# Splitting the two VectorE instructions of a gate chunk into two jobs of the written order

## The reference, cut to what matters

```python
def _L0_ffn_ref(x, w_gate, w_up, w_down):
    wg = _dequant(w_gate, x.dtype); wu = _dequant(w_up, x.dtype); wd = _dequant(w_down, x.dtype)
    gate = jnp.einsum('bsd,hd->bsh', x, wg)
    up = jnp.einsum('bsd,hd->bsh', x, wu)
    h = jax.nn.silu(gate) * up
    return jnp.einsum('bsh,dh->bsd', h, wd)
x = L0_attn_a_x                                        # 8 batches x 256 rows x 128, fp32
x = x + _L0_attn_a_ref(_layernorm(x, axis=-1), ...)    # spike-timing attention, sigmoid projections
x = x + _L0_ffn_ref(_layernorm(x, axis=-1), ...)       # "F": 128 -> 384 -> 128, int weights / 127
x = x + _L0_attn_b_ref(_layernorm(x, axis=-1), ...)    # causal softmax attention, 16 heads of 64
x = x + _L0_ffn_ref(_layernorm(x, axis=-1), ...)       # "P": the same weights again
return x
```

## Time and profile before

| what | us |
|---|---|
| median of 3 runs | 320.98 |
| lowest and highest | 320.28, 321.02 |
| span of the profiled execution | 318.3 |
| TensorE busy (matmuls, modelled ends) | 307.6 |
| TensorE weight loads | 268.4 |
| VectorE busy | 278.0 |
| ScalarE busy | 248.9 |
| GpSimd busy | 227.9 |

### The profile page before, as it was taken

The page is one execution under the profiler, slowest core; times in us unless marked ns, Lnnn a source line. Parts: engine busy times, 40 slices in busy tenths (PEclk is TensorE's granted clock), DMA queues, the critical chain, the costliest instruction groups (busy, mean ns, idle before and its releaser), DMA issues.

```text
span 318.3 us, 10097 instructions
## 1 busy us (share of the span) xinstructions
PE 307.6 (97%) x3186; PEld 268.4 (84%) x3186; DVE 278.0 (87%) x1117; ACT 248.9 (78%) x848; POOL 227.9 (72%) x305
## 2 busy tenths in 40 slices
PE   6898999999999999999999999999999999999995
PEld 5687987988888898898888897888978998888884
DVE  4698999999899989997999989989998898998564
ACT  2665599899779798869889886998779788779832
POOL 4465786949978976977995489863977497646740
PEclk9999999999999999999999999999999999999999
DMA  7900000000000000000000000000000000000001
GB/s 201 316 7 0 3 0 4 2 3 1 2 2 2 2 2 4 0 3 3 18 2 3 3 16 3 2 18 3 2 1 4 19 0 21 2 2 4 2 0 49
DMA packets 6419, 5.83 MB, mean 18 GB/s; under 512 B 864, under 2 KB 5856, under 8 KB 6368
## 3 DMA queue, kind: packets, MB, share of 16 engines
q1 hardware_dynamic: 6080, 4.99, 5.2%
q10 hardware_dynamic: 288, 0.20, 0.2%
HBM read 4.15 MB, written 1.05 MB: 16 GB/s over the span
## 4 chain that ended last, share of the span: by engine, by line
PE 72%; POOL 13%; issue 7%; DVE 5%; DMA 1%; ACT 1%; POOLq 0%; DVEq 0%; ACTq 0%
PE bank L606 10%; PE bank L399 8%; PE bank L400 7%; PE bank L583 7%; PE bank L401 7%; PE bank L571 7%; POOL prob L1019 6%; PE bank L568 4%; PE bank L469 3%; PE bank L459 3%; PE bank L460 2%; PE bank L417 2%; PE bank L448 2%; PE bank L526 2%; PE bank L527 2%
## 5 line engine op out<-in xcount | busy, mean ns | idle before, releaser
L1019 POOL TENSOR_TENSOR prob<-prob,row_inv 128x256 f32<-128x256 f32 (+1 forms) x128 | 103.5, 838 | 33.9 <-DVE row_inv L921 33.8
L719 ACT ACTIVATE prob<-neg_s,neg_max 128x256 f32<-128x256 f32 x128 | 64.1, 501 | 0.0
L717 ACT ACTIVATE prob<-neg_s,neg_max 128x128 f32<-128x128 f32 x128 | 50.8, 397 | 13.8 <-DVE neg_max L897 13.2
L897 DVE CUSTOM_DVE_ANT_0 neg_s<-bank,mask 128x256 f32<-128x256 f32 x128 | 53.7, 420 | 0.0
L606 PE MATMUL bank<-early,v 128*64 128x256 f32 (+1 forms) x512 | 46.0, 330 | 0.1
L606 PEld LDWEIGHTS bank<-early,v 128*64 128x64 f32 x512 | 32.2, 137 | 13.1 <-issue 3.4
L931 DVE TENSOR_TENSOR qk<-bank,bqk 128x512 f32<-128x512 f32 x64 | 42.0, 681 | 0.9 <-PE bank L401 0.8
L571 PE MATMUL bank<-qk 64*128 64x256 f32 x256 | 38.6, 377 | 0.0
L895 DVE CUSTOM_DVE_ANT_0 neg_s<-bank,mask 128x128 f32<-128x128 f32 x128 | 36.4, 284 | 1.8 <-PE bank L571 1.7
L399 PE MATMUL bank<-rt_hi,wqkv_hi 128*128 128x256 f32 x128 | 37.2, 290 | 0.1
L400 PE MATMUL bank<-rt_hi,wqkv_lo 128*128 128x256 f32 x128 | 36.1, 282 | 0.0
(11 more groups left out here) (178 smaller groups left out, 887.2 us busy)
## 6 DMA issues: line engine op xcount, KB each, us to landing
early<-wqkv_in SPq DMA_DIRECT2D x3, 512.0 KB, 6.9
x<-x_in SPq DMA_DIRECT2D x8, 128.0 KB, 5.7
out<-x SPq DMA_DIRECT2D x8, 128.0 KB, 1.8
wo<-wo_in SPq DMA_DIRECT2D x1, 512.0 KB, 7.0
wa<-wa_in ACTq DMA_DIRECT2D x1, 192.0 KB, 3.1
first<-wg_in SPq DMA_DIRECT2D x1, 192.0 KB, 3.1
first<-wu_in SPq DMA_DIRECT2D x1, 192.0 KB, 3.1
first<-wd_in SPq DMA_DIRECT2D x1, 192.0 KB, 4.8
```

The lines of the kernel that those rows point to most:

```text
L717: nc.scalar.activation(prob[:, r, e, 0:P], neg_s[:, m % SCORE_BUFS, e, 0:P], ACT.Exp, bias=neg_max[:, q, 2 * e:2 * e + 1], scale=-1.0, acc ...
L719: nc.scalar.activation(prob[:, r, e, P:SC], neg_s[:, m % SCORE_BUFS, e, P:SC], ACT.Exp, bias=neg_max[:, q, 2 * e + 1:2 * e + 2], scale=-1. ...
L897: nc.vector.tensor_tensor_reduce(out=neg_s[:, m % SCORE_BUFS, e, P:SC], in0=S[:, P:SC], in1=mask[:], scale=-SCORE_SCALE, scalar=3e38, op0= ...
L1019: nc.gpsimd.tensor_tensor(pr, pr, inv, ALU.mult).then_inc(p_norm, 1)
```

## The change

In VectorE's order each `g` job that held both instructions becomes a `g` job with the first and a `u` job with the second. The first increments a semaphore of its own (`silu_s`, one for each feed-forward and chunk), and the `u` job waits for that in place of `link`. For 26 chunks `u` follows its `g` directly. For 18 the first half of another gate chunk, where one followed, now stands between the two halves (`gF1.2 gF2.2 uF1.2 uF2.2`), and for 4 (`gF2.1`, `gP0.0`, `gP2.4`, `gP1.4`) a reciprocal that followed. Nothing else in this order moves, and the orders of the other engines stay as they are.

```diff
-        gF1.0 gF2.0 w0.0 sign.1 lntA.2 ...
+        gF1.0 uF0.0 gF2.0 uF1.0 uF2.0 w0.0 sign.1 lntA.2 ...
-        lntF.1 mask.2 qk.3 qk.4 qk.5 inverse.0 gF2.1 inverse.1 gF1.1 gF0.1 mask.3 ...
+        lntF.1 mask.2 qk.3 qk.4 qk.5 inverse.0 gF2.1 inverse.1 uF2.1 gF1.1 gF0.1 uF1.1 uF0.1 mask.3 ...
-        inverse.9 sum.5 lntF.2 qk.12 sum.7 qk.13 qk.14 gF1.2 gF2.2 mask.12 inverse.10 gF0.2 mask.13 ...
+        ... qk.14 gF1.2 gF2.2 uF1.2 uF2.2 mask.12 inverse.10 gF0.2 uF0.2 mask.13 ...
-        ... mask.19 pt1.16 gF1.3 gF0.3 sum.15 qk.20 qk.21 gF2.3 qk.22 ...
+        ... mask.19 pt1.16 gF1.3 gF0.3 uF1.3 uF0.3 sum.15 qk.20 qk.21 gF2.3 uF2.3 qk.22 ...
-        ... gP0.3 gF0.6 dbP.2 qk.43 pt1.38 pt1.39 inverse.41 gF2.6 gF1.6 sum.37 ...
+        ... gP0.3 gF0.6 uP0.3 uF0.6 dbP.2 qk.43 pt1.38 pt1.39 inverse.41 gF2.6 gF1.6 uF2.6 uF1.6 sum.37 ...
-        ... gP1.4 inverse.51 gF2.7 gF0.7 gF1.7 pt1.48 ...
+        ... gP1.4 inverse.51 uP1.4 gF2.7 gF0.7 uF2.7 gF1.7 uF0.7 uF1.7 pt1.48 ...
...
-        gate_s = {k: [sem(f"gate_s_{k}{c}") for c in range(FC)] for k in "FP"}
+        gate_s, silu_s = ({k: [sem(f"{n}_{k}{c}") for c in range(FC)] for k in "FP"} for n in ("gate_s", "silu_s"))
...
                     h = hid[buffers(k, b)][:, c, :]
-                    link(nc.vector.scalar_tensor_tensor(h, gate_t[buffers(k, b)][:, c, :], 1.0, src[:, 0:N], ALU.add, ALU.mult))
+                    nc.vector.scalar_tensor_tensor(h, gate_t[buffers(k, b)][:, c, :], 1.0, src[:, 0:N], ALU.add, ALU.mult).then_inc(silu_s[k][c], 1)
+                elif job[0] == "u":
+                    k, c = job[1], int(job[2])
+                    src, _, free = home(f"g{k}{c}", b)
+                    dve.wait_ge(silu_s[k][c], b + 1)
+                    h = hid[buffers(k, b)][:, c, :]
                     nc.vector.tensor_tensor(h, h, src[:, N:2 * N], ALU.mult).then_inc(free, 1)
```

More of the change, by code:

```diff
@@ L113 @@
         lnsA.0 ga.0 xnA.0 lnsA.1 lntA.0 gb.0 mean.0 sign.0 lntA.1 w4.0 wf.0 aout.0 lnsF.0 lnsA.2 xnF.0 bv.0 lntF.0 mean.1 gF0.0
-        gF1.0 gF2.0 w0.0 sign.1 lntA.2 dbF.0 lnsB.0 w2.0 xnB.0 lnsA.3 lntB.0 aout.1 lnsF.1 bo.0 qk.0 qk.1 qk.2 mask.0 mask.1
-        lntF.1 mask.2 qk.3 qk.4 qk.5 inverse.0 gF2.1 inverse.1 gF1.1 gF0.1 mask.3 inverse.2 mask.4 mask.5 inverse.3 qk.6 mean.2
-        qk.7 dbF.1 pt1.0 pt1.1 pt1.2 inverse.4 lnsB.1 pt1.3 mask.6 sign.2 mask.7 lntB.1 lntA.3 aout.2 inverse.5 sum.1 sum.3
@@ L117 @@
[L117 to L136, removed]
+        gF1.0 uF0.0 gF2.0 uF1.0 uF2.0 w0.0 sign.1 lntA.2 dbF.0 lnsB.0 w2.0 xnB.0 lnsA.3 lntB.0 aout.1 lnsF.1 bo.0 qk.0 qk.1 qk.2
@@ new lines @@
+        mask.0 mask.1 lntF.1 mask.2 qk.3 qk.4 qk.5 inverse.0 gF2.1 inverse.1 uF2.1 gF1.1 gF0.1 uF1.1 uF0.1 mask.3 inverse.2
+        mask.4 mask.5 inverse.3 qk.6 mean.2 qk.7 dbF.1 pt1.0 pt1.1 pt1.2 inverse.4 lnsB.1 pt1.3 mask.6 sign.2 mask.7 lntB.1
+        lntA.3 aout.2 inverse.5 sum.1 sum.3 inverse.6 qk.8 lnsF.2 inverse.7 qk.9 qk.10 qk.11 pt1.4 pt1.5 pt1.6 pt1.7 mask.8
+        mask.9 mask.10 mask.11 inverse.8 lnsA.4 inverse.9 sum.5 lntF.2 qk.12 sum.7 qk.13 qk.14 gF1.2 gF2.2 uF1.2 uF2.2 mask.12
@@ new lines @@
+        inverse.10 gF0.2 uF0.2 mask.13 mean.3 inverse.11 pt1.8 pt1.9 lnsA.5 sign.3 qk.15 dbF.2 inverse.12 inverse.13 lnsB.2
+        pt1.10 pt1.11 sum.9 mask.14 mask.15 pt1.12 lntB.2 otr.0 aout.3 lnsP.0 sum.11 lntA.4 qk.16 qk.17 lnsF.3 pt1.13 mask.16
+        inverse.14 mask.17 qk.18 lntP.0 inverse.15 inverse.16 lntF.3 qk.19 sum.13 gP2.0 uP2.0 pt1.14 pt1.15 mask.18 inverse.17
+        mask.19 pt1.16 gF1.3 gF0.3 uF1.3 uF0.3 sum.15 qk.20 qk.21 gF2.3 uF2.3 qk.22 inverse.18 pt1.17 lntA.5 mask.20 mask.21
@@ new lines @@
+        inverse.19 gP1.0 uP1.0 dbF.3 lnsB.3 gP0.0 inverse.20 uP0.0 mask.22 pt1.18 pt1.19 otr.1 lntB.3 mean.4 inverse.21 qk.23
+        qk.24 qk.25 lnsP.1 inverse.22 sign.4 pt1.20 mask.23 pt1.21 mask.24 lnsA.6 sum.17 mask.25 inverse.23 aout.4 lntP.1 sum.19
+        sum.21 inverse.24 lnsF.4 gP2.1 uP2.1 qk.26 qk.27 pt1.22 pt1.23 pt1.24 mask.26 mask.27 lntF.4 qk.28 inverse.25 qk.29
+        lnsA.7 gP1.1 uP1.1 qk.30 qk.31 mask.28 inverse.26 gF1.4 uF1.4 mean.5 gF0.4 uF0.4 pt1.25 gF2.4 uF2.4 sum.23 inverse.27
@@ new lines @@
+        sign.5 lntA.6 gP0.1 uP0.1 sum.25 dbP.0 dbF.4 inverse.28 lnsB.4 mask.29 mask.30 otr.2 lnsP.2 inverse.29 pt1.26 pt1.27
+        mask.31 inverse.30 lntB.4 aout.5 lnsF.5 sum.27 qk.32 qk.33 pt1.28 pt1.29 pt1.30 mask.32 mask.33 lntF.5 inverse.31 qk.34
+        qk.35 gF2.5 gF0.5 uF2.5 uF0.5 mask.34 mask.35 pt1.31 qk.36 qk.37 inverse.32 inverse.33 inverse.34 gF1.5 uF1.5 lntP.2
+        mask.36 mask.37 sum.29 sum.31 inverse.35 lntA.7 pt1.32 pt1.33 qk.38 qk.39 gP0.2 uP0.2 dbP.1 gP2.2 uP2.2 dbF.5 inverse.36
@@ new lines @@
+        lnsB.5 inverse.37 pt1.34 pt1.35 mean.6 gP1.2 uP1.2 otr.3 sign.6 lnsP.3 sum.33 pt1.36 pt1.37 lntB.5 sum.35 mask.38
+        mask.39 aout.6 lnsF.6 qk.40 qk.41 lntP.3 mask.40 inverse.38 inverse.39 mask.41 inverse.40 lntF.6 qk.42 gP0.3 gF0.6 uP0.3
+        uF0.6 dbP.2 qk.43 pt1.38 pt1.39 inverse.41 gF2.6 gF1.6 uF2.6 uF1.6 sum.37 pt1.40 pt1.41 sum.39 mask.42 mask.43 qk.44
+        qk.45 gP1.3 uP1.3 dbF.6 lnsB.6 mask.44 inverse.42 inverse.43 mask.45 gP2.3 uP2.3 mean.7 qk.46 qk.47 inverse.44
+        inverse.45 lntB.6 mask.46 otr.4 pt1.42 sign.7 pt1.43 pt1.44 lnsP.4 mask.47 sum.41 qk.48 aout.7 qk.49 lnsF.7 pt1.45
@@ L137 @@
+        mask.48 mask.49 inverse.46 inverse.47 lntP.4 qk.50 qk.51 lntF.7 gP2.4 inverse.48 uP2.4 pt1.46 pt1.47 gP0.4 uP0.4 sum.43
+        sum.45 inverse.49 mask.50 mask.51 dbP.3 sum.47 qk.52 qk.53 inverse.50 gP1.4 inverse.51 uP1.4 gF2.7 gF0.7 uF2.7 gF1.7
+        uF0.7 uF1.7 pt1.48 pt1.49 mask.52 mask.53 otr.5 pt1.50 lnsP.5 qk.54 pt1.51 qk.55 dbF.7 lnsB.7 mask.54 mask.55 inverse.52
         inverse.53 lntB.7 dbP.4 sum.49 sum.51 lntP.5 qk.56 qk.57 inverse.54 inverse.55 qk.58 pt1.52 pt1.53 mask.56 mask.57
-        pt1.54 inverse.56 pt1.55 gP0.5 qk.59 mask.58 pt1.56 sum.53 sum.55 qk.60 qk.61 inverse.57 inverse.58 qk.62 mask.59
@@ L139 @@
-        mask.60 mask.61 qk.63 inverse.59 inverse.60 gP2.5 pt1.57 pt1.58 mask.62 inverse.61 mask.63 pt1.59 otr.6 inverse.62
-        lnsP.6 inverse.63 gP1.5 pt1.60 pt1.61 pt1.62 pt1.63 lntP.6 out0.7 out1.7 lnsP.7 gP1.6 xnP.7 gP0.6 lntP.7 gP2.6 gP0.7
-        gP2.7 gP1.7 dbP.5 dbP.6 dbP.7
+        pt1.54 inverse.56 pt1.55 gP0.5 uP0.5 qk.59 mask.58 pt1.56 sum.53 sum.55 qk.60 qk.61 inverse.57 inverse.58 qk.62 mask.59
+        mask.60 mask.61 qk.63 inverse.59 inverse.60 gP2.5 uP2.5 pt1.57 pt1.58 mask.62 inverse.61 mask.63 pt1.59 otr.6 inverse.62
@@ L142 @@
+        lnsP.6 inverse.63 gP1.5 uP1.5 pt1.60 pt1.61 pt1.62 pt1.63 lntP.6 out0.7 out1.7 lnsP.7 gP1.6 uP1.6 xnP.7 gP0.6 uP0.6
+        lntP.7 gP2.6 uP2.6 gP0.7 uP0.7 gP2.7 uP2.7 gP1.7 uP1.7 dbP.5 dbP.6 dbP.7
     """,
```

## The result

The changed kernel takes 322.08 us (median of 5 runs, 321.95 to 322.13) against 321.02 (320.28 to 321.18) for the kernel before in the same comparison. The ratio is 1.0039, with a 95% interval of 1.0028 to 1.0050: slower by 1.06 us, where +1.1 was forecast (322.1). The main term came as written down. Two smaller terms did not, and the runs of before turned out to have a spread of their own, for which two traces suggest a cause.

The account below looks back on a forecast made before the run. TensorE, nearly without holes from 30 to 300 us, was taken as the bound. Start 0.21, batch 1 -0.10, batch 2 0.87 and batch 6 0.16 sum to +1.14 us, on 320.98 giving 322.1, range 320.5 to 323.0.

Parts of the forecast that it names:

- TensorE is full from 30 to 300 us, and what it loses stays lost: TensorE, 268.86 busy of 270 us: no spare time afterwards, so any delay is kept to the end.
- A covered wait saves 0.11 us: VectorE gate chunks: 0.45 us between dependent halves against 0.34 back to back; ideal saving 2.3 us in all.
- the rival that took it for the path: No saving at all: first halves start 0.45 apart, not 0.34; +0.44 over four places, 322.5 us; chance 0.05.
- Side by side chunks cost nothing: The 26 chunks whose two jobs stay adjacent on VectorE: only the semaphore's name changes, cost zero.
- Batch 2, +0.87, through hid_hi, hid_lo and wo_lo: The main term: uF1.2 behind gF2.2 runs 0.87 us later, delaying hid_hi, hid_lo, wo_lo and TensorE's otA.0 by 0.87.
- a wait of about 1.1 before L526: Expected sign in TensorE's profile: this wait grows to about 1.1 us from 0.28, the longest of the middle.
- Batch 6, +0.16 at gP1.3: uF2.6 0.34 later delays hid_hi, zt_hi, zt_lo and VectorE's mask; less 0.18 slack, TensorE's gP1.3 loses 0.16 us.
- Start, +0.21: Batch 0 F chunks: VectorE's block ends at 24.14, past w0's start at 23.93; +0.21 us on the path, bounds 0 and 0.21.
- Batch 1, -0.10: Three chunks with tanh long ready save 0.3 us on VectorE at 43 us; -0.1 taken, bounds 0 and -0.3.
- new waits elsewhere of over 0.3: Sign that the prediction is wrong: TensorE gets waits above 0.3 us in places not forecast.
- The absorbed case: Rival: after late otA.0, small holes close, batch 1 saving counts, gP1.3 term may vanish; +0.4, 321.4 us; chance 0.28.
- the case of more late banks: Rival: two more bank delays of 0.2 and the batch 3 lag of 0.23; +1.8, 322.8 us; chance 0.10.

Follow-up runs that it names:

- e5: Only the two batch 6 pairs (P0.3 with F0.6, F2.6 with F1.6) interleaved, all other chunks side by side; 321.11 us, ratio 1.0017 to the kernel before.
- e1: Changed kernel with both halves of all 48 chunks side by side again, new semaphores kept; 320.91 us, ratio 1.0005 to the kernel before.
- e2: Only the batch 2 pair F1.2, F2.2 interleaved, the other 46 chunks side by side; 321.70 us, ratio 1.0037 to the kernel before.
- e4: Changed kernel with GpSimd's job ol.0, which makes wo_lo, moved ahead of norm.8; 321.03 us, ratio 1.0016 to the kernel before.
- e11: Changed kernel, all pairs interleaved, with wo_lo made early and VectorE's sign.7 moved behind pt1.44; 320.14 us, ratio 0.9994 to the kernel before.
- e3: Changed kernel with only F1.2 and F2.2 put back side by side; 321.08 us, ratio 1.0014 to the kernel before.
- e6: Changed kernel with VectorE's job sign.7 moved behind pt1.43 and pt1.44; 321.26 us, ratio 1.0021 to the kernel before.
- e9: Only the three chunks of batch 0 interleaved, all else side by side; 320.40 us, ratio 1.0000 to the kernel before.
- e8: Side by side except three groups (F2.1 with a reciprocal, F1.1 with F0.1, F2.5 with F0.5), wo_lo early, sign.7 late; 319.31 us, ratio 0.9962 to before.
- e10: All second halves side by side, wo_lo made early, sign.7 behind pt1.44; 319.48 us, ratio 0.9974 to the kernel before.
- e7: All second halves side by side, GpSimd's wo_lo job moved ahead of norm.8; 319.97 us, ratio 0.9976 to the kernel before.

## Why the prediction was right, point by point

- *TensorE is full from 30 to 300 us, and what it loses stays lost.* Right. In the changed kernel otA.0 stands 0.85 late and dnF.6, 140 us on, 0.88 late (1.12 and 1.15 less 0.27).
- *A covered wait saves 0.11 us.* Right. Two halves in a row are shown as 0.72 to 0.75 us of VectorE for both, which is 0.33 and one whole duration (211.46 in e5). The Trainium skill's rule (VectorE: DVE Perf Modes, section "The DRAIN you can't avoid") that leaving out waits in a chain gains nothing does not hold here (0.33 to 0.34 us from start to start in place of 0.45), and the rival that took it for the path is out. That the saving reaches nobody was right too.
- *Side by side chunks cost nothing.* Right (e1).
- *Batch 2, +0.87, through hid_hi, hid_lo and wo_lo.* Right: 0.87 alone (e2), gone when wo_lo is moved (e4). The sign "a wait of about 1.1 before L526" came as 0.77, because TensorE's jobs in front of it came 0.35 late: the delay by the bank, which the prediction rightly put inside the new wait, shortens the wait that is seen. That this delay is a cost of its own once wo_lo is out of the way (e4, e11) it did not say.
- *Batch 6, +0.16 at gP1.3.* The place and the chain were right, the size was short: 0.16 to 0.18 at gP1.3's first matmul, and 0.07 to 0.08 more before its second (0.20 us after the first, where before it was 0.12), in each kernel with these pairs (dnF.6 to qk.46: 0.25 in the changed kernel, 0.25 in e3, 0.24 in e5). Another 0.1 comes at gP1.4 in e3, e4, e5 and the changed kernel, and not in e6 and e11, which have the same pairs and no meeting at sign.7; so it seems to need both, and what makes it stays open.
- *Start, +0.21.* Wrong. VectorE's block did end later, but the lower bound held. These are its lines after:

```profile
23.42 0.42 DVE L881 SCALAR_TENSOR_TENSOR hid_F<-gate_t_F,bank 128x256 f32<-128x256 f32 x1 [0.36 <-ACT gate_t_F L666]
23.75 0.75 DVE L887 TENSOR_TENSOR hid_F<-hid_F,bank 128x256 f32<-128x256 f32 x2
24.42 0.76 DVE L822 TENSOR_TENSOR wqkv_lo<-early,wqkv_hi 128x512 fp32r<-128x512 f32 x1
25.10 1.76 DVE L892 SCALAR_TENSOR_TENSOR less<-less,dist 128x512 f32<-128x512 f32 x1
```

w0 starts 0.49 later than in the earlier trace rows, 0.22 of it from the change, and takes 0.76 in place of 0.97; sign.1 starts 0.28 later, which is the shift of the first microseconds alone. The same contention with GpSimd, which had stretched w0, gave the time back (e9: 0.77 us for w0, nothing lost): in every trace w0 ends 0.55 us after the GpSimd instruction beside it, whether it starts early or late. The sign "L399 moved to about 27.2" did come (27.25), but by luck, from the difference of the first 8 us.
- *Batch 1, -0.10.* Wrong in size: mean.2 came 0.12 us early and qk.7, three microseconds on, did not. The gain goes at dnF.1 in front of it, whose first matmul is 0.08 early and whose second is not; what holds that job was not read.
- *The sum.* +1.14 was forecast, +1.06 measured. Start and batch 1 were 0.11 too much together, batch 6 and gP1.4 about 0.18 too little. That they nearly cancel is luck. The forecast of the span, 319.5, failed: it was 320.3. The 2.7 us that I put around the span were too much: the execution that was profiled before was one with the race at sign.7 won, and the changed kernel's 322.13 us run has a span of 320.3, so 1.8 us lie around it. The time came out because the sum was added to a median and the changed kernel loses that race in its profile, as most runs behind the median of before seem to. That was luck too.
- *The signs of being wrong.* One of them came: "new waits elsewhere of over 0.3". TensorE waits 0.7 us before transposes.45 (L585), and the prediction has no term for it. It does not speak against the mechanism, since the same wait stands in e1 (0.8), where the order is that of before; but only that experiment could tell.
- *The absorbed case and the case of more late banks.* Neither: no later hole gave anything back, and e3 leaves 0.17 for the other eleven groups (seven of gate chunks, four with a reciprocal).

## What to carry to other kernels

On an engine that runs in order, moving a job behind another one gives it the other's wait as well. So before two chains are interleaved, compare when the second one's input is ready with when it would be reached, pair by pair. Covering a latency of 0.11 us was worth 0.2 us at most on an engine that isn't the bound, even where nothing was held back (e8 against e10), while one late result in front of a long one-time job (here 2.4 us of wo_lo) costs all of its delay; such a job belongs into an idle stretch (0.8 us less here, e7 against e1). And where repeated runs of a kernel fall on two levels, or two traces of the same order part at one place, look for a race between two engines: compare the durations of the same instruction in both.

## What the runs showed of the hardware that was not expected

One VectorE instruction, 512 columns with two SBUF inputs, takes 0.68 us alone. When it loses to a GpSimd instruction that has both inputs in SBUF too, it takes 1.59 to 1.68 us (at 230 us), 1.42 to 1.44 (at 193 us) or 1.75 to 1.76 (at 25 us), and each time it ends 0.55 us after the other has ended. GpSimd's takes 1.50 in place of 1.05 us when that one loses, and ends 0.90 us after VectorE's. So it is not a sharing of speed: the second does most of its work after the first is through. Which one is first can't be read from the starts in the profile: with 0.076 and 0.077 us ahead VectorE fell on either side, and that decided 0.6 us of the kernel's time.
